# GpSimd takes over the key searches' subtractions, and two masks, a map and two scalings change place

## The reference, cut to what matters

```
sim = einsum('pbthn,hkpn->pbthk', q, keys)          # two halves x and y, 4 heads, 64 keys each
scores_xy, idx_xy = top_k(sim, 8)
all_scores = sx[..., :, None] + sy[..., None, :]     # 64 sums; the best 8 are kept
scores, pk = top_k(all_scores, 8)
w = silu(einsum('btd,bthkd->bthk', x, down[idx]) * softmax(scores))
experts = einsum('bthk,bthkd->btd', w, up[idx])
out = x + layernorm(dense + experts)
```

## Time and profile before

| | |
|---|---|
| median of three runs | 2789.25 us |
| the profiled execution: its time, its span | 2791.39 us, 2789.7 us |
| PE, DVE, POOL, ACT busy, share of the span | 95%, 86%, 74%, 63% |
| mean granted TensorE clock | 0.989 of full |
| largest waits of PE's matmuls | L1604 for DVE L1275, 44.1 us; L1434 for DVE L1104, 39.2 us |
| the same of DVE | L1104 for ACT L783, 120.2 us; L1142 for PE L1552, 103.0 us |

### The profile page before, as it was taken

How to read it: one execution, slowest core, us unless ns; L and a number is a source line. 1 busy time by engine, 2 the same in 40 slices (tenths; PEclk the granted TensorE clock), 3 DMA queues, 4 the chain that set the end, 5 groups by cost and what they waited for, 6 DMA issues and landing times. The chain is left out here.

```text
span 2789.7 us, 49914 instructions
## 1 busy us (share of the span) xinstructions
PE 2641.5 (95%) x14624; PEld 2173.9 (78%) x14688; DVE 2396.5 (86%) x5638; ACT 1750.7 (63%) x3688; POOL 2058.8 (74%) x2880
## 2 busy tenths in 40 slices
PE   5999999999999999999999999999999999999985
PEld 4778877878877878877878877878877878877873
DVE  4588889988889988889988889988889888889885
ACT  4566666666666666666666666666666666666653
POOL 3367787877787877787877777877777877777866
PEclk9999999999999999999999999999999999999998
DMA  3000000000000000000000000000000000000000
GB/s 135 8 9 12 5 8 11 11 11 11 4 8 11 11 11 11 4 8 11 11 11 11 0 11 11 11 11 11 0 11 11 11 11 9 2 11 11 8 5 8
DMA packets 28182, 34.23 MB, mean 12 GB/s; under 512 B 2672, under 2 KB 27248, under 8 KB 27440
## 3 DMA queue, kind: packets, MB, share of 16 engines
q1 hardware_dynamic: 28144, 33.77, 3.7%
HBM read 25.37 MB, written 8.39 MB: 12 GB/s over the span
## 5 line engine op out<-in xcount | busy, mean ns | idle before, releaser
L1104 DVE SCALAR_TENSOR_TENSOR acc<-bank,cw,acc 128x253 f32<-128x253 f32 x1920 | 770.4, 470 | 120.8 <-ACT acc L783 120.2
L1434 PE MATMUL bank<-hT,w_in 128*128 128x256 f32 x2560 | 607.5, 383 | 40.0 <-DVE acc L1104 39.2
L620 POOL TENSOR_TENSOR Em<-ee 128x1024 f32<-128x1024 f32 x256 | 562.0, 2215 | 64.9 <-DVE yv L1145 53.6
L1434 PEld LDWEIGHTS bank<-hT,w_in 128*128 128x128 f32 x2560 | 481.1, 191 | 156.7 <-DVE acc L1104 54.0
L1266 DVE SCALAR_TENSOR_TENSOR Em<-Em,p 128x1024 f32<-128x1024 f32 x256 | 429.6, 1678 | 1.7 <-POOL Em L620 1.7
L917 ACT ACTIVATE Em<-Em,rden 128x1024 f32<-128x1024 f32 x256 | 293.0, 1145 | 113.6 <-DVE Em L1275 113.5
L635 POOL TENSOR_TENSOR W<-W,Em 128x1024 f32<-128x1024 f32 x128 | 330.6, 2583 | 8.5 <-ACT Em L917 0.3
L783 ACT ACTIVATE acc<-bank,cb,cw 128x253 f32<-128x253 f32 x640 | 323.5, 559 | 0.0
L1275 DVE TENSOR_TENSOR Em<-Em,products 128x1024 f32<-128x1024 f32 x256 | 310.7, 1214 | 4.6
L1604 PE MATMUL products<-w_de,h2T 128*128 128x512 f32 x512 | 239.0, 610 | 44.2 <-DVE Em L1275 44.1
L1619 PE MATMUL bank<-h2T,w_up 128*128 128x256 f32 x1024 | 242.2, 379 | 1.4 <-ACT sim L887 0.7
(11 more groups left out here) (199 smaller groups left out, 5342.3 us busy)
## 6 DMA issues: line engine op xcount, KB each, us to landing
x_in<-x_dram SPq DMA_DIRECT2D x32, 256.0 KB, 2.7
x_res<-x_dram SPq DMA_DIRECT2D x32, 256.0 KB, 2.7
out_dram<-f SPq DMA_DIRECT2D x32, 256.0 KB, 2.2
w_in<-in_wT_dram SPq DMA_DIRECT2D x1, 3080.0 KB, 12.3
w_up<-upT_dram SPq DMA_DIRECT2D x1, 1024.0 KB, 15.1
w_de<-down_eT_dram SPq DMA_DIRECT2D x1, 1024.0 KB, 17.1
w_down<-downT_dram SPq DMA_DIRECT2D x1, 1024.0 KB, 19.1
w_ue<-up_e_dram SPq DMA_DIRECT2D x1, 1024.0 KB, 21.2
```

Of the source, the lines that this page charges most:

```text
L620: nc.gpsimd.tensor_tensor(Em[:, k], bc(ee[:, k, 0:XD], 2, KEYS), bc(ee[:, k, XD:XD + KEYS], 1, XD), ALU.mult).then_inc(E_done.sem, 1)
L1104: ins = V.scalar_tensor_tensor(acc[:, r, a, TAPS - 1:], ps[:, a * TOK + k:(a + 1) * TOK - TAPS + 1 + k], cw[:, t, k:k + 1], acc[:, r, a, T ...
L1434: last = mm(ring[j % 2][:, a * TOK:(a + 1) * TOK], w_in[:, k, at:at + P], hT[:, k, :], start=k == 0, stop=k == DK - 1)
```

## The change

- VectorE's four subtractions of each `ffn_best` go. GpSimd makes the same four in a new step `ffn_args(e, c)`, for chunk 0 between `mixer_parts` and `mixer_head`, for chunk 1 behind `mixer_head`. VectorE signals the largest values with `best_done` and the indices with `index_done`; GpSimd signals the arguments with `earg_done`.
- GpSimd waits for `rden_done`, the end of the choice, ahead of `mixer_scale(g, 0)`. Before, the first wait for it was one step later, at `weigh(e, 0, 0)`.
- `weigh(e, 1, 0)` moves behind `mixer_root_y(g)`, and its wait for the gate (`y_done`) goes.
- On VectorE `ffn_mask(e, 0, 3)` moves up behind `ffn_mask(e, 0, 2)`, and `ffn_store(f)` stands between these two and `ffn_times(e, 0, 2)`.
- On ScalarE `tail_keep` moves from the end of a group to the next group, behind pairs 0 and 1.

```
+            def ffn_args(e, c):
+                pool.wait_ge(best_done.sem, best_done.at(e, c * RH + RH - 1))
+                if c == 0 and later(e):
+                    pool.wait_ge(E_done.sem, E_done.at(e - 1, CH * RH - 1))
+                rows = ee[:, c * RH:(c + 1) * RH]
+                nc.gpsimd.tensor_tensor(rows[:, :, XD:XD + KEYS], sim[:, c, 1], bc(s8[:, c, 1, :, 0], 2, KEYS),
+                                        ALU.subtract).then_inc(own_pool, own.one())
+                nc.gpsimd.tensor_tensor(rows[:, :, 0:XD], sim[:, c, 0, :, 0:XD], bc(s8[:, c, 0, :, 0], 2, XD),
+                                        ALU.subtract).then_inc(own_pool, own.one())
+                for s in range(2):
+                    at = XD + KEYS + s * TOP
+                    nc.gpsimd.tensor_tensor(rows[:, :, at:at + TOP], s8[:, c, s], bc(s8[:, c, s, :, 0], 2, TOP),
+                                            ALU.subtract).then_inc(own_pool, own.one())
+                pool.wait_ge(own_pool, own.n)
+                pool.sem_inc(earg_done.sem, 1)
...
                     mixer_parts(g)
+                if b:
+                    ffn_args(e, 0)
+                if a:
                     mixer_head(g)
+                if b:
+                    ffn_args(e, 1)
...
+                if b:
+                    pool.wait_ge(rden_done.sem, rden_done.at(e))
                 if a:
                     mixer_scale(g, 0)
...
-                if b:
-                    weigh(e, 1, 0, gate=g)
                 if a:
                     mixer_root_y(g)
+                if b:
+                    weigh(e, 1, 0)
+                if a:
                     tail_root3(g)
...
+                    act.wait_ge(index_done.sem, index_done.at(e - 1, c * RH + RH - 1))
...
                 pairs(0, 1)
                 if c:
+                    tail_keep(f)
                     ffn_experts(f, 0, 3)
...
                     ffn_experts(e, 0, 2)
-                    tail_keep(e)
...
-                V.tensor_tensor(rows[:, :, 0:XD], sim[:, c, 0, :, 0:XD], bc(s8[:, c, 0, :, 0], 2, XD),
-                                ALU.subtract).then_inc(own_dve, own.one())
-                for s in range(2):
-                    at = XD + KEYS + s * TOP
-                    V.tensor_tensor(rows[:, :, at:at + TOP], s8[:, c, s], bc(s8[:, c, s, :, 0], 2, TOP),
-                                    ALU.subtract).then_inc(own_dve, own.one())
-                V.tensor_tensor(rows[:, :, XD:XD + KEYS], sim[:, c, 1], bc(s8[:, c, 1, :, 0], 2, KEYS),
-                                ALU.subtract).then_inc(earg_done.sem, 1)
...
                 if b:
                     ffn_mask(e, 0, 2)
+                    ffn_mask(e, 0, 3)
+                if c:
+                    ffn_store(f)
+                if b:
                     ffn_times(e, 0, 2)
-                if c:
-                    ffn_store(f)
-                if b:
-                    ffn_mask(e, 0, 3)
                 if a:
                     tail_sum(g)
```

More of the change, by code:

```diff
@@ L271, in sandwich @@
         up_ps, up_done = sig("up_ps", FT // 2), sig("up_done", FT // 2)
+        best_done, index_done = sig("best_done", CH * RH), sig("index_done", CH * RH)
         earg_done, ee_done, rden_done = sig("earg_done", CH), sig("ee_done"), sig("rden_done")
@@ L606, in tail_root4, with weigh @@
                 nc.gpsimd.tensor_tensor(shift4[:], rs4[:], neg_mean4[:], ALU.mult).then_inc(root4.sem, 1)
-            def weigh(e, c, *heads, gate=None):
-                if gate is not None:
-                    pool.wait_ge(y_done.sem, y_done.at(gate, CH - 1))
+            def ffn_args(e, c):
[13 more added lines that the diff above has]
+                pool.sem_inc(earg_done.sem, 1)
+            def weigh(e, c, *heads):
                 for h in heads:
@@ L1189, in ffn_best @@
                 dve.wait_ge(sim_sb.sem, sim_sb.at(e, c))
+                if later(e):
+                    dve.wait_ge(earg_done.sem, earg_done.at(e - 1, c))
                 dve.sem_inc(arrived_dve, 1)
@@ L1192, in ffn_best @@
                     for h in range(RH):
-                        V.max(s8[:, c, s, h, :], sim[:, c, s, h, :]).then_inc(own_dve, own.one())
+                        ins = V.max(s8[:, c, s, h, :], sim[:, c, s, h, :])
+                        ins.then_inc(own_dve if s == 0 else best_done.sem, own.one() if s == 0 else 1)
                 dve.wait_ge(own_dve, own.n)
@@ L1196, in ffn_best @@
                     V.max_index(i8[:, c * RH + h, :], s8[:, c, 0, h, :], sim[:, c, 0, h, :])\
[L1197 to L1200, removed]
-                V.tensor_tensor(rows[:, :, 0:XD], sim[:, c, 0, :, 0:XD], bc(s8[:, c, 0, :, 0], 2, XD),
-                                ALU.subtract).then_inc(own_dve, own.one())
-                for s in range(2):
-                    at = XD + KEYS + s * TOP
-                    V.tensor_tensor(rows[:, :, at:at + TOP], s8[:, c, s], bc(s8[:, c, s, :, 0], 2, TOP),
-                                    ALU.subtract).then_inc(own_dve, own.one())
-                V.tensor_tensor(rows[:, :, XD:XD + KEYS], sim[:, c, 1], bc(s8[:, c, 1, :, 0], 2, KEYS),
-                                ALU.subtract).then_inc(earg_done.sem, 1)
+                        .then_inc(index_done.sem, 1)
                 if c == CH - 1:
-                    dve.wait_ge(own_dve, own.n)
+                    dve.wait_ge(index_done.sem, index_done.at(e, CH * RH - 1))
                     V.tensor_copy(i8b[:], i8[:]).then_inc(own_dve, own.one())
@@ L1348, in do_group @@
                     ffn_mask(e, 0, 2)
-                    ffn_times(e, 0, 2)
+                    ffn_mask(e, 0, 3)
                 if c:
@@ L1352, in do_group @@
                 if b:
-                    ffn_mask(e, 0, 3)
+                    ffn_times(e, 0, 2)
                 if a:
```

## The result

Four runs of the changed kernel took 2719.82 to 2721.78 us, median 2721.12 us; the kernel before took 2788.1 to 2790.22 us beside it, median 2788.8 us. The ratio is 0.9756, 95% interval 0.9739 to 0.9773. By its outcome this is rival 1, no wait left at either place, but not by its reason and not by its size (2741 us).

What follows compares the result with a forecast made beforehand. TensorE was taken as the bound, busy 81.49 of 83.80 us. -1.02 + 0.87 = -0.15 us a group, -4.4 us over 29 groups, with +1.5 us for leaks, gave 2788.5 us profiled, 2786 us median; range 2738 to 2798 us.

Steps and rivals of the forecast that it cites:

- rival 1: End of the group: store gets in before GpSimd's map, both TensorE waits vanish, -1.74 us a group, 2741 us; chance 0.34.
- The subtractions and the first wait: Chunk 0, ahead of pair 9: without VectorE's subtractions the convolution comes earlier and TensorE's wait goes, -1.02 us a group.
- Their price on GpSimd: Four subtractions ahead of and behind GpSimd's head: 1.5 us for four, 0.65 for the wide one, hidden, cost nothing.
- Scaled inputs behind the choice: Middle of the group: GpSimd's wait shifts turns, VectorE loses 0.97 us, covered by 1.03 us idle before the second gate.
- The end of the group: Second wait, TensorE's products: root beats mask 3, the map gets in before the store and holds it, +0.87 us a group.
- tail_keep: ScalarE, moved behind pair 1: delays GpSimd and the residual 0.75 us; cost nothing, with thin cover of 0.2 us.
- The sum: Whole group: -1.02 + 0.87 = -0.15 us, -4.4 us over 29 groups; last groups +-1.5 us, leaks +1.5 us.
- my order of events: End of the group: root, power, then map ahead of the store, which takes 2.4 us; forecast 2786 us, chance 0.48.
- Rival 2: GpSimd's head becomes the bound if the four subtractions take over 1.7 us; 2805 us at 2.4 us; chance 0.18.

Runs made afterwards that it cites:

- experiment 1: Kernel before with only the four subtractions moved from VectorE to GpSimd; 2749.44 us, ratio 0.9856.
- experiment 3: Changed kernel without GpSimd's wait for the end of the choice ahead of the scaled inputs; 2721.24 us, ratio 0.9754.
- experiment 12: Changed kernel with ScalarE's tail_keep back at its old place, the end of the group before; 2721.33 us, ratio 0.9761.
- experiment 4: Changed kernel with VectorE's old order at the end of the group (mask 2, times 2, store, mask 3); 2805.01 us, ratio 1.0053.
- experiment 9: Kernel of experiment 4 with TensorE's eight small dt matmuls moved ahead of the second pair of w_in matmuls; 2769.53 us, ratio 0.9937.
- experiment 7: Changed kernel with TensorE's eight small dt matmuls done twice; 2748.67 us, ratio 0.9853.

## Why the prediction was wrong, point by point

- **The subtractions and the first wait**: right in mechanism (experiment 1), too small in size. The step priced it at the idle column, 1.02 us; the timeline's starts gave 1.17, and pair 9's own matmuls 0.11 more. Experiment 1 has 1.30 for the whole term.
- **Their price on GpSimd**: right. 1.28 us where 1.5 was taken, 0.63 us for the wide one where 0.65 was, and hidden.
- **Scaled inputs behind the choice**: right in the order of turns and in "cost nothing" (experiment 3). The gate was held, the middle shifted, and the idle time ahead of the second gate, 1.03 us before, is 0.30 in the trace of the changed kernel: 0.73 us were used up where 0.97 were forecast, and the cover held.

```profile
1066.44 0.69 DVE L1167 TENSOR_TENSOR yv<-yv,bank 128x512 f32<-128x512 f32 x1 [0.30 <-PE bank L1569]
```

- **The end of the group**: this is the step that failed. "It ends at 1097.40, the power at 1098.15, and the map is asked for at 1098.15": I gave the power the 0.70 us of the earlier trace rows and let only the root stand in VectorE's way. The root did come in unheld (0.19 us). But the power has operands in SBUF too and was held by mask 3 for 0.88 us. This put the map behind the store, and the sign of the term turned: the group got 0.93 us of VectorE's time back, 0.80 of it at the first mask, and did not lose 0.87. The row that misled me is free for another reason: in the earlier trace rows no mask runs when the power asks, because the old order has times there. I had moved that mask myself in the same paragraph. (The same paragraph's 0.15 us before a mask's end doesn't follow from its root of 0.25 us, which gives 0.20; with the 0.19 us measured it is 0.14, and the order of events is the same by either.)
- **tail_keep**: right, nothing (experiment 12).
- **The sum**: with the tail's sign right, the two idle columns give 29 x 1.74 = 50 us and, with the 2 us that rival 1 takes off for the head, its 2741 us. The repetition gave 2.17 us, 29 x 2.17 = 63 us. The measured gain is 68 us, and 72 between the two profiled executions. Of these 72, 61 lie in the 28 steady repetitions, 5.7 in the first three and 5.5 behind the last dt matmuls, where the prediction had +-1.5 in all. Part of it may be chance: the first three repetitions of experiment 12, a kernel of the same time, are 2.4 us longer than the changed kernel's. I did not take the ends apart. So besides the sign, the size of each wait was too small, by 0.15 us at each of the two places, and the matmuls behind them gave another 0.14.
- **What would have come of my order of events**: experiment 4 has it, and it is not 2786 us. The waits alone make it 2769.5 (experiment 9); with the clock it is 2805. Both terms of "-1.02 + 0.87 = -0.15 us a group" were off: experiment 9 has 83.17 - 83.84 = -0.67, and as pair 9 gives -1.30 (experiment 1), the products cost +0.63. The store took 2.11 us, not 2.4, and the wait was 1.34 us by the idle column, not 1.59. The forecast had no term for the clock either, and the clock was worth 35.5 us (experiment 4 against experiment 9). The Trainium skill's sentence ("SBUF — State Buffer", section "SBUF: two separate sides"), that whichever starts first gets the pair for the whole instruction, agrees with these traces where GpSimd's instruction is a long one: VectorE's was stretched to between 1.93 and 2.19 us here. For the short ones it does not: the power and the store overlap by 0.64 us in the changed kernel, both unlengthened once the mask had gone. I applied it to the root and the store and not to the power between them.

Rival 2 had nothing: the head is waited for on ScalarE, but TensorE's waits behind it did not grow.

## What to carry to other kernels

When an edit moves one engine's long instructions, take every instruction of the other engine that now falls among them, small ones too, and ask again whether its duration in the old trace was a free one. Price a wait of TensorE from start to start against the matmuls' own step, not by the idle column alone, and look at the granted clock behind it: here a wait of 1.5 us cost 3.2 in the groups in which the clock fell. Edits that share such turns don't add up (1.4% slower alone, 1% faster together with another), so each has to be tried on top of the others.

## What the runs showed of the hardware that was not expected

- TensorE's granted clock fell within a group, from its upper level to the lower one for 3.4 us, which cost 1.7 us each time (85.6 against 83.9 us, 84.9 against 83.2). What the engine had done before, from start to start with the idle column in brackets: it stood for 2.10 us (1.95) between wide matmuls; for 1.49 us (1.34) next to eight small ones; for 0.61 us (0.45) next to sixteen small ones. It did not fall when it had stood for 1.48 us (1.24) between wide matmuls, for 1.18 us (1.03) next to eight small ones, or for 1.17 us (1.02) between wide ones, nor with sixteen small ones and no wait (experiment 7). What decides between them, and why one repetition in three to five was spared, is open.
- More matrix work made the kernel faster: 1.7 us of wide matmuls a group, 2828.6 to 2790.6 us. Small ones did not (2805.0 to 2805.8), though the busy column counts both alike.
- A GpSimd power on two columns, 0.70 us, takes 1.58 us when it asks 1 us before the end of a VectorE mask. That is longer than the wide subtraction, so a small operand buys no place in the turn. Freed by the mask, it ran beside a VectorE store of 0.69 us that reads SBUF too, and neither was lengthened.
- The idle column of pipelined matmuls counts to a modelled end. At pair 9 it had 1.02 us where the starts have 1.17, at the products 0.72 where the next trace gave back 0.87.
